# A decoder block in fp32 on one core: GpSimd's low parts of weight chunks wait for VectorE's normalisation, the first batch's corrections for the last rope low part

## What is computed

```python
q, k, v = x @ w_q, x @ w_k, x @ w_v          # 32 query heads, 8 key/value heads of 128
lk, lv = (x @ w_lq) @ w_lk, x @ w_lv         # 32 latent heads
q, k, lk = rope(q), rope(k), rope(lk)
attn = causal_attn(q, repeat(k), repeat(v)) @ w_o + causal_attn(q, lk, lv) @ w_lo
x1 = layernorm(x + attn)
x2 = layernorm(x1 + fake_quant(x1) @ fake_quant(ctx))   # 8-bit grid, context 1024 x 1024
out = layernorm(x2 + fp8_scaled(x2) @ fp8_scaled(w))    # scale and clip only
```

## Time and profile before

| | us |
|---|---|
| median of 3 runs | 2453.62 (2452.92 to 2454.64) |
| profiled execution: its time | 2453.53 |
| profiled execution: its span | 2451.7 |
| TensorE busy | 2440.1 (100% of the span) |
| VectorE busy | 1724.6 (70%) |
| ScalarE busy | 1116.6 (46%) |
| GpSimd busy | 894.9 (37%) |

### The profile page before, as it was taken

How to read it: one execution, slowest core, us unless ns; L and a number is a source line. 1 busy time by engine, 2 the same in 40 slices (tenths; PEclk the granted TensorE clock), 3 DMA queues, 4 the chain that set the end, 5 groups by cost and what they waited for, 6 DMA issues and landing times.

```text
span 2451.7 us, 40455 instructions
## 1 busy us (share of the span) xinstructions
PE 2440.1 (100%) x12324; PEld 2066.0 (84%) x12324; DVE 1724.6 (70%) x3603; ACT 1116.6 (46%) x2564; POOL 894.9 (37%) x676
## 2 busy tenths in 40 slices
PE   9999999999999999999999999999999999999999
PEld 7888888888888888888878888888888888888877
DVE  7767767677675767766787676776767576667666
ACT  4544445354444435344554444535344453544551
POOL 4343342424334242433533434253343425334210
PEclk9999999999999999999999999999999999999999
DMA  6232232323223231323423323232232323234411
GB/s 203 69 88 72 75 97 60 105 58 92 66 78 94 65 104 55 97 62 108 135 88 118 94 83 102 73 109 64 88 90 81 104 72 109 67 87 146 161 35 69
DMA packets 122823, 222.06 MB, mean 91 GB/s; under 512 B 12912, under 2 KB 21232, under 8 KB 122608
## 3 DMA queue, kind: packets, MB, share of 16 engines
q1 hardware_dynamic: 117536, 211.93, 28.8%
q10 hardware_dynamic: 5200, 9.18, 1.1%
HBM read 202.18 MB, written 18.87 MB: 90 GB/s over the span
## 4 chain that ended last, share of the span: by engine, by line
PE 95%; DVE 3%; issue 1%; ACT 1%; DMA 0%; SPq 0%; DVEq 0%; ACTq 0%
PE bank_a L1368 16%; PE bank_a L1370 16%; PE bank_a L1369 16%; PE bank_b L1369 13%; PE bank_b L1370 13%; PE bank_b L1368 13%; PE bank_b L1430 5%; PE bank_b L1757 1%; PE bank_a L1503 1%; PE bank_b L1692 0%; DVE q_lo L902 0%; DMA w_raw<-wstream 0%; DVE probs L895 0%; DVE probs L894 0%; PE bank_b L1740 0%
## 5 line engine op out<-in xcount | busy, mean ns | idle before, releaser
L478 POOL TENSOR_TENSOR w_lo<-w_raw,w_hi 128x512 fp32r<-128x512 f32 x612 | 815.4, 1341 | 1359.6 <-ACT w_hi L550 1337.5
L550 ACT ACTIVATE w_hi<-w_raw 128x512 fp32r<-128x512 f32 x616 | 383.3, 627 | 263.1 <-DMA w_raw<-wstream 131.4
L592 ACT ACTIVATE probs<-probs,row_min 128x512 f32<-128x512 f32 (+3 forms) x512 | 282.2, 553 | 474.5 <-DVE row_min L912 474.5
L1368 PE MATMUL bank_a<-w_hi,o_hi 128*128 128x512 f32 x1024 | 414.3, 405 | 1.4 <-DVE o_lo L934 1.4
L1370 PE MATMUL bank_a<-w_hi,o_lo 128*128 128x512 f32 x1024 | 400.8, 391 | 0.0
L1369 PE MATMUL bank_a<-w_lo,o_hi 128*128 128x512 f32 x1024 | 399.7, 390 | 0.0
L929 DVE TENSOR_TENSOR pT_lo<-bank_b,pT_hi 128x512 fp32r<-128x512 f32 (+1 forms) x384 | 207.2, 595 | 180.5 <-ACT pT_hi L598 180.5
L923 DVE TENSOR_SCALAR probs<-probs,row_inv 128x512 f32<-128x512 f32 (+3 forms) x512 | 256.5, 561 | 4.5
L1370 PEld LDWEIGHTS bank_a<-w_hi,o_lo 128*128 128x128 f32 x1024 | 192.2, 188 | 41.5
L912 DVE CUSTOM_DVE_ANT_0 probs<-bank_b,mask_sb 128x512 f32<-128x512 f32 (+3 forms) x512 | 221.5, 482 | 5.1 <-PE bank_b L1370 3.9
L1368 PEld LDWEIGHTS bank_a<-w_hi,o_hi 128*128 128x128 f32 x1024 | 193.0, 189 | 34.7 <-DVE o_lo L934 2.4
(11 more groups left out here) (206 smaller groups left out, 4767.3 us busy)
## 6 DMA issues: line engine op xcount, KB each, us to landing
w_raw<-wstream SPq DMA_DIRECT2D x615, 256.0 KB, 2.7
stage<-ctx SPq DMA_DIRECT2D x32, 256.0 KB, 2.7
stage_w<-wf SPq DMA_DIRECT2D x32, 256.0 KB, 2.8
q_scratch<-stage_q SPq DMA_DIRECT2D x32, 128.0 KB, 1.7
wf_hi_scratch<-piece_hi SPq DMA_DIRECT2D x16, 256.0 KB, 2.9
wf_lo_scratch<-stage_w SPq DMA_DIRECT2D x16, 256.0 KB, 3.3
wf_hi<-wf_hi_scratch SPq DMA_DIRECT2D x8, 512.0 KB, 7.0
wf_lo<-wf_lo_scratch SPq DMA_DIRECT2D x8, 512.0 KB, 8.3
```

The lines of the kernel that those rows point to most:

```text
L478: nc.gpsimd.tensor_tensor(w_lo[:, s], w_raw[:, r], w_hi[:, s].bitcast(F32), ALU.subtract).then_inc(lo_done, 1)
L550: nc.scalar.activation(w_hi[:, s], w_raw[:, r], ACT.Copy).then_inc(hi_done, 1)
L592: nc.scalar.activation(part, part, ACT.Exp, bias=row_min[:, u % 2, i:i + 1], scale=-1.0, accum_out=row_sum[:, u % 2, i:i + 1]).then_inc(ex ...
L1368: nc.tensor.matmul(dst, still[0], move[0], start=start, stop=False)
```

## The change

GpSimd gets a new helper before each low part. For chunks 27 to 37 it waits until VectorE has normalised unit u = (c - 26) // 2 of the same group; in the first group of a batch only chunks 30 and up wait. Chunks 0 to 3 of groups 1 to 7 wait for units 6 and 7 of the group before. Besides, in G=8 the corrections at c = 22 and after wait for all nine rope low parts.

```diff
@@ -496,15 +496,29 @@
+            def behind_normalisation(G, c, first):
+                u = (c - C_PREV - AHEAD) // 2
+                if c > C_PREV + AHEAD and not (first and c < C_OWN):
+                    pool.wait_ge(normed, 4 * (UNITS * G + u + 1))
+                elif c < AHEAD and not first:
+                    pool.wait_ge(normed, 4 * (UNITS * (G - 1) + UNITS - 2 + c // 2 + 1))
+
             def group(b, g, first):
                 G = g + KVH * b
                 for c in range(CHUNKS):
+                    behind_normalisation(G, c, first)
                     low(b, g, c, c)
...
+                    if b and first and c == C_PREV:
+                        pool.wait_ge(rope_lo, ROPES * (G + 1))
                     if b and first and C_PREV <= c < C_PREV + TT:
                         add_corr(c - C_PREV, corr0)
```

## The result

The changed kernel takes 2459.03 us in the median of 20 runs (2457.64 to 2461.47); the kernel before, on the same chip, takes 2453.48 (20 runs, 2452.44 to 2456.51). The ratio is 1.0022 [1.0016, 1.0028]: 5.5 us slower. The profiled execution took 2458.3 us, its span 2456.5, which is 4.8 more than before's span. The two traces differ by 0.7 us before any new wait can act: TensorE's first scores of G=0, near 65 us, come 0.7 earlier than before's. Over the other runs of this study this start varies from 0.9 earlier to 0.75 later, so it belongs to no edit. Taken from the first scores on, the change costs 4.8 + 0.7 = 5.5 us, as the medians say.

The account below looks back on a forecast made before the run. TensorE was taken as the bound, with 95% of the chain and full windows in fourteen groups. 5.7 + 1.7 - 0.6 - 0.3 + 0 = +6.5 on the profiled 2453.53 gave 2460.0 us, range 2457.2 to 2463.0.

Parts of the forecast that it names:

- rival A: The forecast: TensorE's stall in G=8 plus a clock fall, 2460.0 us (2458.8 to 2462.3), chance 0.50.
- Part 2: Second batch's first group: TensorE wants chunk 30 before unit 2's normalisation lets its low part run; stall +5.7 us (5.3 to 6.2).
- Part 3: Behind the G=8 stall TensorE may return at its lower clock level: +1.7 us, bounds 0 and 2.6.
- Part 4: Time given back by VectorE's relief: one-column maximum in G=0 -0.6 us, normalisation before o_lo in G=8 -0.3 us.
- Part 5: G=8 corrections after the last rope low: 0.6 us gained at lv_lo, given back at the cross residual; 0 (-0.7 to +0.5).
- Part 1: Gate in ordinary groups: low parts have over 10 us slack, cost 0; shorter normalisations gain 0, covered by TensorE's full windows.
- so they start 0.2 us later: G=8: ScalarE's exponentials wait for all four corrections, ending at 1239.7; their table load stood at 1239.48.
- B: Same G=8 stall but TensorE's clock stays up: 2458.3 us (2457.3 to 2459.0), chance 0.30.
- C: Not slower: VectorE's relief ends unit 2's normalisation early enough that the gate costs nothing; 2451.9 us, chance 0.04.
- E: Waits are already met whenever GpSimd reaches them, nothing changes: 2453.6 us, chance 0.04.
- D: Delayed low parts also starve the w_raw ring, 0.3 us in each of 14 groups, on top of B: 2462.5, chance 0.12.
- the prediction's own signs of being wrong: G=8 wait under 4 us, TensorE gaps in ordinary groups, or ScalarE's w_hi waiting for DMA more than now.

Follow-up runs that it names:

- the last experiment: Changed kernel without the gate for chunks 30 and 31, tail's first chunks gated, all-reduce moved behind the tail's fourth low part: 2454.72 us, ratio 1.0002.

## Why the prediction was right

The forecast, rival A with 2460.0 (2458.8 to 2462.3), holds: 2459.03 in the median, and both of its mechanisms are there. Its sum was +6.5 on the profiled time, the two spans show +4.8, and 0.7 of the difference is the start-up scatter. By its steps, each measured as the shift of TensorE's marks between the two traces:

| step | predicted | measured |
|---|---|---|
| chunk 30's wait in G=8, stall (Part 2) | +5.7 | +5.6 |
| clock behind it (Part 3) | +1.7 | +1.5 |
| one-column maximum in G=0 (Part 4) | -0.6 | -0.65 |
| o_lo in G=8 (Part 4) | -0.3 | -0.15 |
| corrections (Part 5) | 0 | -0.7 |
| 14 ordinary groups (Part 1) | 0 | -1.4 |
| end of the first batch (in no part) | not foreseen | +1.55 |
| later scores in G=0, scores behind the slow matmuls (in no part) | not foreseen | -0.3 |
| sum | +6.5 | +5.5 |

The measured column comes from one pair of traces. Steps of 0.1 us are alike in all groups and in the other traces with the gate; a place where nothing was edited can still move by 0.8 us between executions, as the experiments with chunk 30 alone and with the corrections alone show.

**Parts 2 and 3** came out by their own working. The chain of residual, pT_lo, normalisation and low part is in the trace in that order, and that unit 2 is normalised after TensorE needs the chunk came from reading the order of parts in a first group. Three corrections of detail. The wait is labelled "issue". The clock's price is not fixed: 1.5 and 2.1 behind this stall, within the bounds of 0 and 2.6. And the upper bound does not hold for every stall: behind that of the last experiment it was 2.8.

**Part 4** held for G=0; in G=8 it gave half of what was put down, within its range. In G=0 the maximum fell from 0.82 us to 0.16 (VectorE's timeline):

```profile
95.31 0.16 DVE L985 TENSOR_TENSOR sc<-sc 128x1 f32<-128x1 f32 x1
95.39 1.61 DVE L943 TENSOR_TENSOR pT_lo<-bank_b,pT_hi 128x512 fp32r<-128x512 f32 x3
```

**Part 5** was wrong in a term. The step that failed is "so they start 0.2 us later": the exponentials' table load, at 1239.48 before, came at 1238.43 in the changed kernel, 1.05 earlier, 0.6 of which the run was ahead already. The low part of the last q ended at 1229.1 and not at 1230.1 (again 0.6 of it from before), so the corrections, whose length of four times 2.38 was right to 0.1 us, ended at 1238.62, while the table load was still running, and were out of the way in time. With that "the 0.6 gained is given back" failed too: VectorE's cross residual began 1.32 us earlier than before, at 1246.22, and TensorE's matmuls around it kept the 0.7. The 0.7 lies at the favourable end of that part's range.

**Part 1** was wrong in both directions. To put the gain at 0 because it is "covered by TensorE's full windows" read the windows too coarsely: a window counts a matmul as busy from its start to its modelled end, and a wait of 0.1 us hides under the end of the matmul before it. The waits of the weight load for pT_lo, before and then in the changed kernel, both from 1290 to 2345 us (us in total, times, longest), show it:

```profile
PEld bank_b L1368 <- DVE pT_lo L929: 2.0, 8, 0.3
```

```profile
PEld bank_b L1382 <- DVE pT_lo L943: 0.4, 2, 0.2
```

The prediction did not use this line. Where it bites is one matmul of scores in each group: the one at 1971.31 lasted 0.49 us before, its counterpart at 1976.37 in the changed kernel 0.39. And "Cost 0" for the chunks of ordinary groups followed the gate to TensorE, which has the slack named, but not along GpSimd's own queue to the all-reduce and to the tail's chunks behind it. The Part listed add_columns and piece_low behind the gated chunks; the all-reduce, 14 us of GpSimd's time, was missing. "The change touches no tail chunk" is true of the code and not of the time at which these chunks run. The two misses, -1.4 and +1.55, cancel by luck, so the total is better than the working.

**The rivals.** B (no clock fall) is excluded by the window at 0.51. C and E are excluded by the stall. D (starved ring) did not come: the experiment with the ordinary groups' gate alone is not slower. Two of the prediction's own signs of being wrong did come, without D's mechanism. ScalarE's w_hi waited 57.8 us for DMA in 1035 us of the second batch's ordinary groups, against 49.6 before; but the kernel with the corrections' wait alone, which has no gate there, shows 57.6, and TensorE met none of it. And TensorE has a gap in an ordinary group, the 1.1 us at the end of G=7, which comes from the low parts beside the last normalisation.

Open: why the trace writes "issue" at the 5.38 us, why GpSimd stands idle around the all-reduce, and what sets the length of the low clock. Not tried: reordering the parts of G=8 so that chunk 30 is wanted later.

## What to carry to other kernels

A gate that ties one engine's work to another's progress is right only for the order of work it was written for: check it in each special case, the first group, the last one and the tail, where the consumer asks in another order. Here a rule that is harmless to the 14 ordinary groups costs some 7 us in one, and leaving two chunks out turns +0.22% into -0.09% (interval up to 0.00%); gating the tail as well makes -0.17%. Follow a delay down the delayed engine's own queue as well as to its consumer, up to rare long instructions such as a partition all-reduce. And price a stall of the bound engine with the slow matmuls behind it.

## What was unexpected of the hardware

- The GpSimd partition all-reduce at the end of the first batch is recorded with 0.4 to 0.7 us, but over the nine traces the engine does nothing for 6.3 to 7.1 us before it and for 6.6 to 8.5 us after it.
- Back-to-back low parts on GpSimd stretch four VectorE normalisations from 1.27 to 3.47 us (changed kernel) and 3.77 us (ordinary groups alone), far more than one low part does.
- Even a one-column VectorE operation suffers: 0.82 us beside a low part, 0.16 without.
- TensorE's granted clock fell to 0.5 behind an idle stretch of 3.62 us as behind one of 5.38, and stayed low for some 3.4 us in the changed kernel and for 6.8 us in two of the experiments.
